# An attention product and a LoRA product on one core: the opening, the x loads' queue and the place of a few steps

## The chip, the cores and the metric

The kernel runs on one core of a Trainium2 chip. Engines of a core run side by side and meet in semaphores: TensorE (PE, with its weight loads as PEld), VectorE (DVE), ScalarE (ACT), GpSimd (POOL), and SyncE (SP), which only issues transfers. Loads and stores run on the core's 16 DMA engines; those that SP issues are on queue q1, those that POOL issues on q0. The metric is the time of one execution in microseconds.

## What is computed

For each of two batches: x is layer-normalised, rounded to integers 0 to 255, and multiplied with a context matrix rounded the same way; the result is added to x. Then the sum is normalised again and goes through a dense layer with a bias and two low-rank (LoRA) corrections, which is added too.

```python
def fake_quant(x, scale, zp):
    q = jnp.clip(jnp.round(x / scale + zp), 0.0, 255.0)
    return (q - zp) * scale
# x (2, 1024, 2048), ctx (2, 2048, 2048), kernel (2048, 2048), 4 of 8 gate rows for each batch
x = x + fake_quant(layernorm(x)) @ fake_quant(ctx)
y = layernorm(x)
x = x + y @ kernel + bias + B_eff @ (A_eff @ y) + lora_B_shared @ (lora_A_shared @ y)
```

## The kernel before

Each batch has 1024 rows, in 8 tiles (t) of 128; the 2048 output columns are 4 blocks (j) of 512; the 2048 deep inner dimension is 4 groups (g) of four 128 x 128 steps. Tile t has PSUM bank t. The first product takes bf16 integers (16 matmuls of 512 columns a tile and block); the second splits both sides into a high and a low fp16 half and takes three matmuls a step (48 a tile and block).

All orders are written out by hand, one program for each engine, and every hand-over is a semaphore. What matters here:

- **The opening** (batch 0, block 0). POOL issues x tiles 0 to 3, then makes the identity and some patterns, then takes roots of variances (`root_one`, `root_pair`). VectorE takes statistics of a tile (`stats1`), its variance (`variance`), scale and shift (`scale_rows`, six small dependent steps for one tile, or for two tiles side by side). ScalarE applies them (`relu_rows`), VectorE rounds (`round1`). Tiles 0 to 3 are turned by TensorE through PSUM (`turn`, copied out by `turn_out`), tiles 4 to 7 by a DMA that SP issues (`turn_q`). Ctx groups 0 and 1 come over SP into the two halves of `stage`, groups 2 and 3 over POOL (`load_head`); ScalarE converts them (`conv_ctx`, `conv_head`) and VectorE rounds them. `first_block` is TensorE's order. A column term (`column_term`, one matmul a tile) closes each tile of batch 0; it needs a row made from the sum over the ctx block (`column_sum`, ScalarE, then VectorE's `column_low`). The products with lora_A and lora_B follow.
- **The last block of the first product** (`first_by_tile`). Its last two tiles (`tail`) run group by group, so that ring slots of the early groups come free sooner. Meanwhile VectorE evicts tiles (`evict1`), normalises and splits the first rows (`norm2`, `low2`), and makes the low halves of the first weight block (`w_group`) after ScalarE's high halves (`conv_w`); SP turns the rows (`turn_high`, `turn_low`) and loads weight groups into `stage`.
- **The second product** starts with `base0_pair` (tiles 0 and 1, group by group) and then one tile after another; the four products with the A matrix of a gate (`lora_in`, 32 matmuls of 256 columns) stand between tiles, the first after the pair.
- **The next batch's x.** While weight blocks 2 and 3 of batch 0 run, batch 1's tiles pass through the one buffer `xn`: load, statistics and normalising (`norm_next`, VectorE), quantising (`quantise_next`, ScalarE), a store to a scratch tensor. Three tiles belong to a block. `load_next_x` issues the load on POOL, between POOL's bias additions (`add_bias`, eight a block) and stores. ScalarE converts the next weight block only after the three tiles.

## Time and profile before

| | us |
|---|---|
| three timed runs | 1040.86, 1041.74, 1045.02 (median 1041.74) |
| the profiled execution | 1042.47 |
| its span, first to last instruction | 1040.9 |
| TensorE busy | 992.6 (95%) |
| VectorE busy | 539.1 (52%) |
| ScalarE busy | 296.1 (28%) |
| GpSimd busy | 216.1 (21%) |
| mean granted TensorE clock | 0.994 of full speed |

Busy shares are means over stages that differ; where TensorE is busy nearly always, a change is worth what it takes out of TensorE's waits. A wait is read from the list of waits (who waited for whom, in total), placed with the timeline, and followed back: what did the instruction that ended it wait for? The granted clock is read by windows; 1.00 is 2.4 GHz, 0.50 is 1.2 GHz.

### The profile page before, as it was taken

The page shows a single profiled execution, that of the slowest core. Times are in us where ns is not written, and L with a number is a line of the kernel's source. Part 1 is how long each engine was busy: PE and PEld are TensorE (multiplying, and loading weights), DVE is VectorE, ACT ScalarE, POOL GpSimd, SP SyncE. Part 2 cuts the span into 40 slices and gives each one's busy share as a digit, 9 for nine tenths or more (in the row PEclk, how much of TensorE's full clock was granted, in tenths as well). Part 3 has the DMA queues.
Part 4 walks back from the last instruction along what each step waited for, and adds up shares of the span by engine and source line. Part 5 has one row for each costly group of instructions (what it writes and reads, how often), then busy time and mean ns, then how long its engine had stood idle before and what let it go on. Part 6 is the DMA issues. An engine that isn't in the chain of part 4 may idle for free.

```text
span 1040.9 us, 11977 instructions
## 1 busy us (share of the span) xinstructions
PE 992.6 (95%) x4640; PEld 460.9 (44%) x4663; DVE 539.1 (52%) x757; ACT 296.1 (28%) x213; POOL 216.1 (21%) x231
## 2 busy tenths in 40 slices
PE   2899999899999989999999999989999999999997
...
GB/s 364 295 247 366 392 295 29 171 163 194 192 223 162 111 167 177 173 146 207 252 261 284 322 198 84 108 145 165 224 118 162 31 101 161 20 33 149 11 31 40
DMA packets 140138, 181.48 MB, mean 174 GB/s; under 512 B 112704, under 2 KB 112960, under 8 KB 127552
## 3 DMA queue, kind: packets, MB, share of 16 engines
...
q0 software_dynamic: 13472, 58.20, 15.7%
...
## 4 chain that ended last, share of the span: by engine, by line
PE 62%; DVE 13%; DMA 8%; ACT 6%; issue 6%; POOL 3%; SPq 0%; DVEq 0%; POOLq 0%; ACTq 0%
PE psum L1029 17%; PE psum L1224 13%; PE psum L1226 13%; PE psum L1225 13%; DMA xn<-in_x 3%; DMA stage<-in_w 3%; POOL x L655 2%; DVE ring L1495 2%; PE psum L1247 2%; DVE hl L1541 2%; ACT ring L807 1%; DMA lhs<-in_lora_b 1%; PE psum L1091 1%; DVE stats L1521 1%; DVE stats L1406 1%
## 5 line engine op out<-in xcount | busy, mean ns | idle before, releaser
L1224 PE MATMUL psum<-ring,lhs 128*128 128x512 f16 x1000 | 379.6, 380 | 8.4 <-DVE ring L1495 7.3
L1226 PE MATMUL psum<-ring,lhs 128*128 128x512 f16 x1000 | 379.8, 380 | 0.0
L1225 PE MATMUL psum<-ring,lhs 128*128 128x512 f16 x1000 | 379.7, 380 | 0.0
L1029 PE MATMUL psum<-ring,lhs 128*128 128x512 bf16 x1002 | 226.8, 382 | 4.5 <-DVE ring L1461 2.0
L1029 PEld LDWEIGHTS psum<-ring,lhs 128*128 128x128 bf16 x1024 | 100.4, 98 | 126.5 <-issue 5.1
L1224 PEld LDWEIGHTS psum<-ring,lhs 128*128 128x128 f16 x1000 | 98.0, 98 | 129.1 <-DVE ring L1495 10.4
L1226 PEld LDWEIGHTS psum<-ring,lhs 128*128 128x128 f16 x1000 | 98.0, 98 | 118.4 <-issue 0.6
L1225 PEld LDWEIGHTS psum<-ring,lhs 128*128 128x128 f16 x1000 | 98.0, 98 | 116.7 <-issue 0.8
L1548 DVE SCALAR_TENSOR_TENSOR x<-psum,sc,x 128x512 f32 (+1 forms) x63 | 44.6, 746 | 194.0 <-PE psum L1236 193.2
L655 POOL TENSOR_TENSOR x<-x,bias_sb 128x512 f32<-128x512 f32 (+1 forms) x64 | 94.0, 1492 | 153.0 <-ACT x L938 123.9
L807 ACT ACTIVATE ring<-stage,sc 128x2048 f16<-128x2048 f32 x32 | 63.6, 1999 | 198.0 <-PE psum L1226 137.5
L1495 DVE SCALAR_TENSOR_TENSOR ring<-stage,sc,ring 128x2048 f16<-128x2048 f32 x32 | 75.0, 2349 | 64.2 <-ACT ring L807 60.8
L795 ACT ACTIVATE ring<-stage,pats_sb,sc 128x2048 int16<-128x2048 f32 x30 | 62.5, 2091 | 88.8 <-DMA stage<-in_ctx_in 47.3
L674 POOL DMA_DIRECT2D out<-x x48 | 26.4, 551 | 236.8 <-DVE x L1548 221.8
L1509 DVE SCALAR_TENSOR_TENSOR x<-psum,sc,x 128x512 f32<-128x512 f32 x64 | 45.3, 743 | 28.4 <-PE psum L1029 12.8
L629 POOL TENSOR_TENSOR x<-x,bias_sb 128x512 f32<-128x512 f32 x32 | 47.3, 1512 | 41.4 <-ACT bias_sb L934 41.4
L1461 DVE TENSOR_SCALAR ring<-ring 128x2048 bf16<-128x2048 int16 x30 | 23.6, 787 | 41.7 <-ACT ring L795 41.5
L1379 DVE BATCH_NORM_STATS2 stats<-xn 128x6 f32<-128x512 f32 x32 | 19.8, 680 | 48.7 <-DMA xn<-in_x 48.6
L783 ACT ACTIVATE hl<-xn 128x2048 f16<-128x2048 f32 x16 | 30.5, 1909 | 44.5 <-DVE xn L1531 42.1
L1541 DVE TENSOR_TENSOR hl<-xn,hl 128x2048 f16<-128x2048 f32 x16 | 36.9, 2304 | 9.1 <-ACT hl L783 8.6
L1501 DVE SCALAR_TENSOR_TENSOR b_st<-stage,sc,b_st 64x1024 f16<-64x1024 f32 x16 | 23.6, 1484 | 33.8 <-ACT b_st L814 33.7
L732 POOL DMA_DIRECT2D out<-x x14 | 7.7, 547 | 121.5 <-DVE x L1548 121.1
...
## 6 DMA issues: line engine op xcount, KB each, us to landing
stage<-in_w SPq DMA_DIRECT2D x38, 1024.0 KB, 7.1
stage<-in_ctx_in SPq DMA_DIRECT2D x30, 1024.0 KB, 7.5
...
x<-in_x POOLq DMA_DIRECT2D x8, 1024.0 KB, 11.8
xn<-in_x POOLq DMA_DIRECT2D x8, 1024.0 KB, 8.0
...
lhs<-in_lora_a POOLq DMA_DIRECT2D x4, 1024.0 KB, 10.0
lhs<-in_lora_b SPq DMA_DIRECT2D x4, 1024.0 KB, 10.2
```

The source lines that it names most:

```text
L629: pool.tensor_tensor(v, v, bias_sb[:, :], ALU.add).then_inc(with_col, 1)
L655: pool.tensor_tensor(v, v, bias_sb[:, :], ALU.add).then_inc(biased, 1)
L795: act.activation(ring_i[:, g, j % 2, :, :], stage[:, i % 2, :, :], ACT.Relu, bias=Z2, scale=IS2).then_inc(act_conv, 1)
L807: act.activation(ring[:, g, 0, :, :], stage[:, i % 2, :, :], ACT.Copy, scale=of_block(CW0, j)).then_inc(act_conv, 1)
L1029: last = pe.matmul(psum[:, t, :], lhs_q[:, k, t * P:(t + 1) * P], ring_q[:, g, j % 2, u, :], start=(k == 0), stop=(k == KT - 1 and not by_pe))
L1224: pe.matmul(psum[:, t, :], hi, ring[:, g, 0, u, :], start=(kk == 0), stop=False)
L1225: pe.matmul(psum[:, t, :], hi, ring[:, g, 1, u, :], start=False, stop=False)
L1226: last = pe.matmul(psum[:, t, :], lo, ring[:, g, 0, u, :], start=False, stop=False)
L1495: dve.scalar_tensor_tensor(out=ring[:, g, 1, :, :], in0=stage[:, half_w(b, g), :, :], scalar=of_block(CW0, j), in1=ring[:, g, 0, :, :], op ...
L1509: dve.scalar_tensor_tensor(out=v, in0=psum[:, t, :], scalar=S12, in1=v, op0=ALU.mult, op1=ALU.add).then_inc(evicted, 1)
L1541: dve.tensor_tensor(hl[:, 1, :], xn[:, :], hl[:, 0, :], ALU.subtract).then_inc(y_lo, 1)
L1548: dve.scalar_tensor_tensor(out=v, in0=psum[:, t, :], scalar=of_block(INVS0, j), in1=v, op0=ALU.mult, op1=ALU.add).then_inc(evicted, 1)
```

## The change

In the opening, x tile 0 is loaded in two halves with a semaphore each; its statistics, ReLU, rounding and turning go by halves. Ctx group 0 moves from SP's queue to POOL's, between x tiles 1 and 2, with a semaphore of its own (`first_in`; `landed` corrects the counts of the other). Each tile gets its own root and its own scale step, with one dependent step fewer (`scale_row`), and the orders of VectorE, ScalarE and TensorE are written anew around that. The column terms of the first block begin after tile 5 instead of tile 4. In the last block of the first product `tail` is 4 instead of 2, for both batches; VectorE's evictions of tiles 2 and 3 stand behind the weight groups; the first `lora_in` stands inside the pair, ahead of group 3. The loads of the next batch's x move from POOL to SP.

```diff
...
             sp.wait_ge(x_in[1], 16)
-            load_ctx(0, 0, [0, 1])
+            load_ctx(0, 0, [1])
...
+            def load_next_x(b, t):
+
+                sp.wait_ge(q_rows, t + SUMS * b)
+                if not isinstance(t, int):
+                    sp.sem_inc(go_sp, 1)
+                sp.dma_start(xn[:, :], x_tile[b][bass.ds(t, 1), :, :].rearrange("a p d -> p (a d)")).then_inc(x_next, 16)
...
+                    for t in range(LNL + 1, TILES):
+                        load_next_x(b, t)
...
+                if b + 1 < NBATCH:
+                    sp.wait_ge(y_lo, TILES * (b + 1))
                 with sp.Fori(2, NBLK) as j:
                     if b == 0:
+                        load_next_x(b + 1, LNB * (j - 2))
                         w_peaks_block(j)
-                    w_block(b, j)
+                        w_block(b, j, [0, 1])
+                        for i in range(1, LNB):
+                            load_next_x(b + 1, LNB * (j - 2) + i)
+                        w_block(b, j, [2, 3])
+                    else:
+                        w_block(b, j)
                     load_b(b, j, 0)
                     load_b(b, j, 1)
+                if b + 1 < NBATCH:
+                    load_next_x(b + 1, LNL)
...
-            def root_pair(p):
-                pool.wait_ge(pair_var, p + 2)
-                pool.tensor_tensor(ROOT2, VEPS2, NEG_HALF, ALU.pow).then_inc(pair_root, 1)
-
-            load_x(range(4))
+                c = i % 2
+                pool.tensor_tensor(ROOT2[:, c:c + 1], VEPS2[:, c:c + 1], NEG_HALF[:, c:c + 1], ALU.pow).then_inc(pair_root, 1)
+
+            pool.dma_start(x2[:, 0, 0:D // 2], x_tile[0, 0, :, 0:D // 2]).then_inc(x_half, 16)
+            pool.dma_start(x2[:, 0, D // 2:D], x_tile[0, 0, :, D // 2:D]).then_inc(x_in[0], 16)
+            load_x([1])
+            pool.dma_start(stage[:, 0, :, :], ctx_v[0, 0, 0]).then_inc(first_in, 16)
+            load_x([2, 3])
...
+            root_one(2)
+            root_one(3)
...
-                if b + 1 < NBATCH:
-
-                    pool.wait_ge(y_lo, TILES * (b + 1))
                 with pool.Fori(1, NBLK - 1) as j:
-                    if b + 1 < NBATCH:
-                        load_next_x(b + 1, LNB * (j - 1))
                     add_bias(b, j, j + blk2(b, 0), True)
                     next_bias(j, j + blk2(b, 0))
-                    if b + 1 < NBATCH:
-                        for i in range(1, LNB):
-                            load_next_x(b + 1, LNB * (j - 1) + i)
                     if b == 0:
                         pool.wait_ge(red_in, j + 4)
                         pool.sem_inc(go, 1)
                         pool.partition_all_reduce(PW_W, MX_W, P, RED.max).then_inc(red_out, 1)
                     store(b, j, j + blk(b, 1, 0))
-                if b + 1 < NBATCH:
-                    load_next_x(b + 1, LNL)
                 add_bias(b, NBLK - 1, blk2(b, NBLK - 1), True)
-                if b + 1 < NBATCH:
-                    for t in range(LNL + 1, TILES):
-                        load_next_x(b + 1, t)
...
+            def relu_half(h):
+                act.wait_ge(normed, 1)
+                cols = slice(h * D // 2, (h + 1) * D // 2)
+                act.activation(q_ints[0][:, cols], x2[:, 0, cols], ACT.Relu, bias=tile_col(SHIFT1, 0),
+                               scale=tile_col(SCALE1, 0)).then_inc(relued if h else half_relued, 1)
...
-            relu_rows(0)
-            relu_rows(1)
+            relu_half(0)
+            relu_half(1)
             turn_out(0, range(2))
             ctx_block(0, 0, [0])
+            relu_rows(1)
+            ctx_block(0, 0, [1])
             turn_out(1, range(2))
-            ctx_block(0, 0, [1])
             relu_rows(2)
+            conv_head(2)
             relu_rows(3)
             turn_out(2, [0])
-            conv_head(2)
+            conv_head(3)
             turn_out(3, [0])
...
                     pe.wait_ge(ident_ready, 1)
-                pe.wait_ge(rounded, t + 1)
                 for h in range(2):
+                    if t == 0 and h == 0:
+                        pe.wait_ge(half_rounded, 1)
+                    else:
+                        pe.wait_ge(rounded, t + 1)
...
+                ring_ready(0, 0, 0)
+                tile_start(0, 0, 0)
+                group1(0, 0, 0, True)
                 turn(1)
+                ring_ready(0, 0, 1)
+                group1(0, 0, 1, True)
+                tile_start(0, 0, 1)
                 for g in range(2):
-                    ring_ready(0, 0, g)
-                    for t in range(2):
-                        if g == 0:
-                            tile_start(0, 0, t)
-                        group1(0, t, g, True)
+                    group1(0, 1, g, True)
                 turn(2)
+                ring_ready(0, 0, 2)
+                for t in range(2):
+                    group1(0, t, 2, True)
                 turn(3)
-                for t in range(2, PT):
-                    tile_start(0, 0, t)
-                    for g in range(2):
-                        group1(0, t, g, True)
-                for g in range(2, NG):
-                    ring_ready(0, 0, g)
-                    for t in range(PT):
-                        group1(0, t, g, True)
+                tile_start(0, 0, 2)
+                for g in range(3):
+                    group1(0, 2, g, True)
+                tile_start(0, 0, 3)
+                for g in range(3):
+                    group1(0, 3, g, True)
+                ring_ready(0, 0, 3)
+                for t in range(PT):
+                    group1(0, t, 3, True)
                 column_sum(0, 0)
...
-                    column_term(0, range(t + 1) if t == PT else [t])
+                    if t > PT:
+                        column_term(0, range(t + 1) if t == PT + 1 else [t])
...
-                tail = 2 if j == NBLK - 1 else 0
+                tail = 4 if j == NBLK - 1 else 0
...
+                    lora_in(b, 0)
                     pe.wait_ge(converted, grp_w(b, 0, 3) + 1)
...
-                lora_in(b, 0)
...
+            def scale_row(t):
+
+                i = t % 2
+                root, veps, t2, scale, shift = [v[:, i:i + 1] for v in (
+                    ROOT2, VEPS2, T2, pair_cols(SCALE1, t // 2), pair_cols(SHIFT1, t // 2))]
+                dve.wait_ge(pair_var, t + 1)
+                dve.wait_ge(pair_root, t + 1)
+                then(dve.scalar_tensor_tensor(out=t2, in0=root, scalar=root, in1=veps, op0=ALU.mult, op1=ALU.mult))
+                then(dve.tensor_scalar(t2, t2, 0.5, -1.5, ALU.mult, ALU.add))
+                then(dve.scalar_tensor_tensor(out=t2, in0=root, scalar=IS1, in1=t2, op0=ALU.mult, op1=ALU.mult))
+                dve.tensor_scalar(scale, t2, -1.0, None, ALU.mult)
+                dve.tensor_scalar(shift, MV2[:, i:i + 1, 0], t2, Z1, ALU.mult, ALU.add).then_inc(normed, 1)
+                dve.wait_ge(normed, t + 1)
+
+            def round_half(h):
+                cols = slice(h * D // 2, (h + 1) * D // 2)
+                dve.wait_ge(relued if h else half_relued, 1)
+                dve.tensor_scalar(q_slots[0][:, cols], q_ints[0][:, cols], 255.0, -CENTRE,
+                                  ALU.min, ALU.add).then_inc(rounded if h else half_rounded, 1)
...
-            stats1(0)
+            stats1(0, range(2))
+            stats1(0, range(2, NBLK))
             variance([0])
+            scale_row(0)
             stats1(1, range(2))
-            scale_rows([0], 0)
-            stats1(1, range(2, NBLK))
+            round_half(0)
+            stats1(1, [2])
+            round_half(1)
+            stats1(1, [3])
             variance([1])
-            round1(0)
             stats1(2, range(2))
-            scale_rows([1], 1)
+            scale_row(1)
+            ctx_group(0, 0, 0)
             stats1(2, range(2, NBLK))
+            variance([2])
             round1(1)
...
+            round1(4)
             stats1(6, range(2))
-            round1(4)
+            scale_row(5)
             stats1(6, range(2, NBLK))
+            variance([6])
             round1(5)
-            stats1(7)
-            variance([6, 7])
-            scale_rows([6, 7], 4)
+            stats1(7, range(2))
+            scale_row(6)
+            stats1(7, range(2, NBLK))
+            variance([7])
             round1(6)
+            scale_row(7)
             round1(7)
...
-                evict1(b, j, 2)
                 norm2(b, 1)
-                evict1(b, j, 3)
                 w_group(b, 0, 0)
                 low2(b, 1)
                 w_group(b, 0, 1)
-                evict1(b, j, 4)
-                evict1(b, j, 5)
-                evict1(b, j, 6)
-                evict1(b, j, 7)
+                for t in range(2, TILES):
+                    evict1(b, j, t)
...
```

VectorE in the opening, tiles 6 and 7 (before; `stats` and `sc` are small tables, `ring` here holds the tile's integers):

```order
L1406 BN_STATS stats<-x 128x6 x4
L1414 BN_AGGR sc<-stats 128x2 x2
L1415 TENSOR_SCALAR sc<-sc 128x2
L1424 TENSOR_TENSOR sc<-sc 128x2
L1425 TENSOR_TENSOR sc<-sc 128x2
L1426 TENSOR_SCALAR sc<-sc 128x2
L1428 SCALAR_TENSOR_TENSOR sc<-sc 128x2
L1429 TENSOR_TENSOR sc<-sc 128x2
L1430 TENSOR_SCALAR sc<-sc,pats_sb 128x2
L1435 TENSOR_SCALAR ring<-ring 128x2048 x2
```

and VectorE at tiles 6 and 7 now:

```order
L1440 BN_STATS stats<-x 128x6 x2
L1458 SCALAR_TENSOR_TENSOR sc<-sc 128x1
L1459 TENSOR_SCALAR sc<-sc 128x1
L1460 SCALAR_TENSOR_TENSOR sc<-sc 128x1
L1461 TENSOR_SCALAR sc<-sc 128x1
L1462 TENSOR_SCALAR sc<-sc,pats_sb 128x1
L1440 BN_STATS stats<-x 128x6 x2
L1448 BN_AGGR sc<-stats 128x2
L1449 TENSOR_SCALAR sc<-sc 128x1
L1473 TENSOR_SCALAR ring<-ring 128x2048
L1458 SCALAR_TENSOR_TENSOR sc<-sc 128x1
```

Two tiles' statistics, one scale step for both and two roundings have become half a tile's statistics, a scale step, the other half, the variance and a rounding, over and over.

TensorE in the pair that opens the second product, after weight group 1 (before, then now; `ap_st` is the A matrix, L1204 and L1235 are weight group 2's high half, L1210 and L1241 its low half, L1224 and L1255 group 3):

```order
L1204 MATMUL psum<-ring,lhs 128x512 x16
L1210 MATMUL psum<-ring,lhs 128x512 x8
L1224 MATMUL psum<-ring,lhs 128x512
L1225 MATMUL psum<-ring,lhs 128x512
L1226 MATMUL psum<-ring,lhs 128x512
L1224 MATMUL psum<-ring,lhs 128x512
```

```order
L1235 MATMUL psum<-ring,lhs 128x512 x16
L1241 MATMUL psum<-ring,lhs 128x512 x8
L1278 MATMUL psum<-lhs,ap_st 128x256 x32
L1255 MATMUL psum<-ring,lhs 128x512
L1256 MATMUL psum<-ring,lhs 128x512
L1257 MATMUL psum<-ring,lhs 128x512
```

The 32 matmuls on the A matrix now stand ahead of group 3.

SP inside the loop over weight blocks 2 and 3, at the loads of weight groups 0 to 3 (before, then now; `REGISTER_ALU` and `ISA` rows are address and semaphore work of the sequencer):

```order
L465 DMA stage<-in_w 128x2048
L461 REGISTER_ALU
L465 ISA
L465 DMA stage<-in_w 128x2048
L461 REGISTER_ALU
L465 DMA stage<-in_w 128x2048
```

```order
L474 DMA stage<-in_w 128x2048
L470 REGISTER_ALU
L474 ISA
L474 DMA stage<-in_w 128x2048
L490 REGISTER_ALU
L493 ISA
L493 DMA xn<-in_x 128x2048
L490 REGISTER_ALU
L493 ISA
L493 DMA xn<-in_x 128x2048
L470 REGISTER_ALU
L474 DMA stage<-in_w 128x2048
```

Two x loads, each with its wait for a quantised tile, stand between weight group 1 and weight group 2; a third stands at the loop's head.

## Rows read from the trace of the kernel before

**Rows 1.** TensorE's waits: line waited for, us in total, times, longest.
```profile
PE psum L1116 <- DVE hl L1435: 15.0, 1, 15.0
PE psum L1224 <- DVE ring L1495: 7.3, 5, 2.6
```

**Rows 2.** Timeline of the opening: start us, us, engine, line, operation, [idle before].
```profile
1.52 2.27 POOL L560 DMA_DIRECT2D x<-in_x  x4 [0.83 <-POOLq L1915]
4.90 0.50 DVE L1738 CAST bias_sb<-bias_sb 128x128 bf16<-128x128 f32 x1 [0.19 <-POOL bias_sb L576]
6.75 2.47 DVE L1406 BATCH_NORM_STATS2 stats<-x 128x6 f32<-128x512 f32 x4 [1.06 <-DMA x<-in_x]
12.07 2.09 ACT L743 ACTIVATE hl<-x,sc 128x2048 int16<-128x2048 f32 x1 [7.12 <-DVE sc L1430]
...
23.98 3.60 PE L1029 MATMUL psum<-ring,lhs 128*128 128x512 bf16 x8 [1.71 <-DVE ring L1461]
47.83 0.16 DVE L1424 TENSOR_TENSOR sc<-sc 128x2 f32<-128x2 f32 x1 [0.87 <-POOL sc L571]
49.14 4.08 ACT L743 ACTIVATE ring<-x,sc 128x2048 int16<-128x2048 f32 x2 [6.16 <-DVE sc L1430]
53.25 0.69 DVE L1435 TENSOR_SCALAR ring<-ring 128x2048 bf16<-128x2048 int16 x1 [1.22 <-ACT ring L743]
54.79 1.25 PE L1064 MATMUL psum<-bias_sb,ones 128*128 128x512 f16 x5 [1.25 <-DVE bias_sb L1456]
66.88 13.90 PE L1091 MATMUL psum<-lhs,pats_sb 128*128 128x512 f32 x32
```

**Rows 3.** DMA issues of 3.3 to 4 us and 52 to 54: KB, us to landing.
```profile
x<-in_x POOLq DMA_DIRECT2D x1, 1024.0 KB, 12.1
...
lhs<-ring SPq DMA_TRANSPOSE x1, 4.6
```

**Rows 4.** Timeline, batch 0, start of the second product, ScalarE and TensorE.
```profile
197.51 2.00 ACT L807 ACTIVATE ring<-stage,sc 128x2048 f16<-128x2048 f32 x1 [12.98 <-DMA stage<-in_w]
...
206.42 0.39 PE L1224 MATMUL psum<-ring,lhs 128*128 128x512 f16 x1 [1.50 <-DVE ring L1495]
211.61 3.66 PE L1247 MATMUL psum<-lhs,ap_st 128*128 128x256 f16 x32
226.14 0.38 PE L1224 MATMUL psum<-ring,lhs 128*128 128x512 f16 x1 [0.52 <-issue]
```

**Rows 5.** Timeline, batch 1, the same place, VectorE and SP.
```profile
664.66 2.35 DVE L1495 SCALAR_TENSOR_TENSOR ring<-stage,sc,ring 128x2048 f16<-128x2048 f32 x1 [2.97 <-PE psum L1029]
...
670.99 1.71 SPq L465 DMA_DIRECT2D stage<-in_w  x2
```

**Rows 6.** DMA issues of 672 to 674 us, the A matrix.
```profile
ap_st<-a_scratch SPq DMA_TRANSPOSE x1, 11.3
```

**Rows 7.** Timeline, boundaries of weight blocks 2 and 3, batch 0.
```profile
316.01 11.82 POOL L655 TENSOR_TENSOR x<-x,bias_sb 128x512 f32 x8 [10.53 <-issue]
...
329.76 0.54 POOL L611 DMA_DIRECT2D xn<-in_x  x1 [0.43 <-issue]
...
341.76 2.47 DVE L1379 BATCH_NORM_STATS2 stats<-xn 128x6 f32<-128x512 f32 x4 [10.68 <-DMA xn<-in_x]
...
372.62 3.90 ACT L807 ACTIVATE ring<-stage,sc 128x2048 f16<-128x2048 f32 x2 [1.32 <-issue]
...
387.35 0.39 PE L1224 MATMUL psum<-ring,lhs 128*128 128x512 f16 x1 [2.61 <-DVE ring L1495]
...
479.63 0.39 PE L1224 MATMUL psum<-ring,lhs 128*128 128x512 f16 x1 [1.48 <-DVE ring L1495]
```

**Rows 8.** Windows: us, TensorE busy, granted clock, DMA share, GB/s.
```profile
68.00:72.00 4.00, 4.00 (x10) 1.00 0.10 12
...
92.00:94.00 2.00, 2.00 (x4) 0.50 0.85 352
...
388.00:390.00 2.00, 2.00 (x6) 0.50 0.56 157
```

79 lines of the change are left out of this document (37 added, 42 removed).

## The prediction

> **What bounds the kernel now.** I read the granted clock first, then TensorE's own waits, then the places where they fall. TensorE is busy 992.6 of the 1040.9 us span, so the kernel is a stream of matmuls with holes, and the change can only act on the holes. The list of TensorE's waits shows the two largest: 15.0 us before its first instruction, and 7.3 us in five waits for VectorE's half of a weight group [rows 1]. Placed in time, these are four stretches. The opening, 0 to 66.9 us, ends where the lora_A products start [rows 2]. At the start of the second product of either batch, weight groups 2 and 3 come late [rows 4] (batch 1 repeats the pattern at 679.8 and 688.7). At the boundary of weight blocks 2 and 3 of batch 0 TensorE waits 2.61 us and 1.48 us [rows 7]. The fourth, the 1.99 us wait in the lora_B products, the change does not address. The granted clock was 0.50 (the lower level, 1.2 GHz) in 388 to 390 us, just after the 2.61 us wait, and there 2 us of stream held 6 matmuls [rows 8]; at the upper level they start 0.216 us apart. That wait thus costs more than itself: ten matmuls from 387.6 to 391.2 us at 0.43 instead of 0.22 us, 2.0 us.
>
> **Part 1, the opening.** I replayed the five engines' orders by hand with the durations of the rows, first for the kernel before (the replay puts the lora_A products at 67.6 us, the trace at 66.9, so it is some 0.7 us late), then for the changed order.
> Tile 0 in halves: four loads took POOL 2.27 us, 0.57 each [rows 2]. There are now six in front of the identity, so VectorE's cast of the identity moves from 4.90 to about 6.0 and its statistics from 6.75 to about 7.0. The first half landing early is therefore worth nothing; VectorE is not there to read it. The scale chain then waits for POOL's root alone and has five steps instead of six (six took 49.14 - 47.83 = 1.31 us [rows 2], so 1.1): ReLU of tile 0 can start at 11.7 instead of 12.07. ReLU in two halves of 1.05 us (half of 2.09) with the roundings between them lets TensorE begin at 13.4 instead of 15.04.
> First ctx group on the x queue: it is fourth there, ahead of x tiles 2 and 3. The fourth transfer of that queue was issued at 3.25 and landed 12.1 us later [rows 3]; x tile 2 now has that place, and its issue is later too, so it lands near 15.7. VectorE wants it at 15.4. ctx group 0 is there before ScalarE is free (16.4), so the first products run near 19.5 instead of 23.98.
> The ring rule of the Trainium skill's page "DMA: Bandwidth & Descriptors" (section "Queues, rings and completion order") speaks against this: one queue's ring starts its descriptors in order, while different queues share the engines in turn, so tile 2 pays for a whole ctx group. No row of before separates order from sharing. By sharing alone tile 2 would land near 11.6 and the opening would be some 0.3 us better.
> A scale per tile: for tiles 4 to 7 each tile now goes through half its successor's statistics (1.3), the scale (1.1), ReLU (2.09) and rounding (0.69) in a ring, 5.0 us a tile with handoffs. Roundings end at 41.0, 46.0, 51.0 and 54.8 us. Before, with pairs, the last ends at 53.25 + 0.69 = 53.9 [rows 2]. The turning DMA lands 4.6 us after its issue [rows 3], so tiles are ready at 45.7, 50.7, 55.7 and 59.5. TensorE, whose column sum now ends near 45.6 instead of 49.9, waits 1.5 us for tile 5. The column term that cost the 1.25 us wait at 54.79 [rows 2] is put off by a tile, but TensorE reaches it at 54.2 and its low row is ready at 55.5: the wait is not gone, it is the same 1.3 us. From there six terms (1.3), tile 6, tile 7 and their terms (7.3) give 64.1 against 67.6 in the replay: 3.5 us. I take **3.0**, because the ring of four tiles has more handoffs than the replay prices. Its bounds are 0.5 above nothing and 4: one more microsecond for tile 2 and half a microsecond per tile on the DMA turns leave 0.5.
> Is it kept to 187 us? The lora_B loads wait for TensorE's own products, and the DMA engines were busy only 0.10 of 68 to 72 us [rows 8], so that train of transfers starts when TensorE says so and moves with it. I keep all 3.0.
>
> **Part 2, the start of the second product.** The tail of the last attention block now runs four tiles group by group instead of two. Group 0 of the ring is released 24 matmuls earlier (5.2 us), group 1 16 matmuls (3.5 us); the block's end does not move. In batch 1 VectorE waited 2.97 us for exactly this release, up to 664.66 [rows 5]; with two evictions also put behind it, the low half of weight group 1 and the issue of weight loads 2 and 3 at 670.99 come 2.2 us earlier (what is then last is the second tile's low half behind its turn). In batch 0 there was no such wait; only the two evictions at 0.67 us each go, so 1.2 us. ScalarE started group 2 at 197.51, released by a load [rows 4], and at 679.8 in batch 1 likewise; both move with it. The 1.13 us wait in batch 0 shrinks to about 0.5, the 1.29 us in batch 1 goes.
> The lora product moved ahead of group 3 (32 matmuls, 3.66 us) is pulled into the 1.50 us wait at 206.42 [rows 4] and its like in batch 1 at 688.7; group 3 is then ready before TensorE asks. The product needs its A matrix: issued at 672.8, landed 11.3 us later at 684.1 [rows 6], now about 681.9, and TensorE arrives at 687.2 - 0.3 - 1.3 = 685.6. Cover 3.7 us; in batch 0 it is 3.3.
> What is late next is tile 3: TensorE waited 0.52 us for its turned halves at 226.14 already [rows 4], and they hang on VectorE's chain, which moves only by 1.2 and 2.2 us. Anything above that which TensorE gains it gives back there. So **1.2** in batch 0 and **2.0** in batch 1. Bounds: 0 (the chain does not move) and 3.3 and 3.1 (all waits of the stretch).
>
> **Part 3, the x loads of the next batch on SP's queue.** On POOL they stood behind work: POOL's eight bias adds ran 316.01 to 327.8, the load was issued at 329.76, and VectorE's statistics waited 10.68 us for it, to 341.76 [rows 7]. Through two such tiles ScalarE is done quantising only at 371.3 and starts weight group 0 at 372.62, and group 2 reaches TensorE at 387.3, 2.61 us late [rows 7]. On SP the first load goes out at 302.9 instead of 304.95 with nothing ahead of it and lands near 309.5 instead of 316.5. The second waits for the quantised tile (322) and for VectorE's maxima (324.1), is issued at 324.6 behind two weight loads and lands by 333, 8.8 us early. The third then lands near 350.6, and quantising ends near 362. Group 0's ring slot is only released 15.5 us before the block's end at 379.6, at 364.1, so ScalarE is no longer what is late. Group 2: load issued 368.5, landed 374.3, both halves done by 379, wanted at 384.8. Group 3: 384 against 387.4. Both waits should close: 2.6 + 2.0 (clock) + 1.5 = **6.1**. What is queued behind the new waits on SP are weight loads 2 and 3, which need group 0 converted anyway, and that is later than the quantising. Lower bound 0, if the x load behind the weight loads is as slow as the 12.0 us it took before. POOL loses the loads; its bias adds start sooner, and nobody waits for them.
> Nothing else has a price: the semaphores' new counts and the wait for y_lo on SP pass when reached.
>
> **Sum.** 3.0 + 1.2 + 6.1 + 2.0 = 12.3 us. The profiled execution took 1042.47 us (1.57 outside its span), 0.7 above the median of the three timed runs, inside their 1040.86 to 1045.02. 1042.5 - 12.3 = **1030.2 us**.
>
> **Rivals.**
> A, the forecast, 1030.2 (1027 to 1033): 45%.
> B, the opening gives nothing: x tile 2 late, the one-tile ring as slow as the pairs, new short holes of TensorE at the lower clock. For it: tile 5's rounding is later than now (46.0 against 43.8). 1030.2 + 3 to 5, 1034: 20%.
> C, everything closes: 3.5 + 3.3 + 6.1 + 3.1, and the lora_B stall no longer drops the clock (in 92 to 94 us it stood at 0.50 [rows 8]; four matmuls at 0.88 for 0.43, 1.8 us): 17.8 off, 1024.7: 12%. Against it: VectorE's chain at tile 3.
> D, the boundary waits stay, since three x loads share SP's ring with six weight loads and the one at 329.76 took 12.0 us beside weight loads already. 1030.2 + 6.1 = 1036.3: 13%. By the ring rule of the same page of the Trainium skill this is the likelier way for the second tile to be late, since it must start after both weight loads.
> E, the other side: the A matrix is turned by a DMA behind two weight loads and TensorE now stands at its product with group 3's matmuls queued behind. It decides once the landing is more than 3.3 us later than I have it; at twice 11.3 us the stall is 7.6 us and 2 us of clock in each batch: 1030.2 + 19 = 1049: 4%.
> F, the change doesn't do what it says, the order moves but the same waits end last: 1041: 6%.
>
> **How the numbers follow.** A measurement here can tell about 0.5% from no change, 5.2 us, so faster means below 1036.5. A, B and C lie there with 77%, and D half: 84% faster. F, the other half of D: 12% the same. E: 4%. The range takes in A to D: 1024.5 to 1037.
>
> **What would show it.** Opening: lora_A products start near 63.9; TensorE's first instruction near 13.4; if the first is above 66, B. Second product: no VectorE wait for the ring before group 0 in batch 1, the A product between groups 2 and 3 without a wait; a wait of 1 to 2 us at tile 3. Boundaries: no wait near 376 and 463, the granted clock 1.00 there, x loads landing in 6 to 9 us. A wait of several us before the lora product would be E. The forecast is wrong above all if the x loads on SP's queue take 12 us.

## The result, and the profile after

The changed kernel took 1031.22 us (median of four runs, 1030.22 to 1032.51) against 1042.53 for the kernel before on the same chip: a ratio of 0.9891 with a 95% interval of 0.9874 to 0.9907. The forecast was 1030.2. Measured again later (experiment 11) it took 1034.53, ratio 0.9929 (0.9908 to 0.9950); why it varies so is part of what follows. The profiled execution took 1032.13 us, its span is 1030.6; TensorE is busy 990.9 of it.

TensorE's largest waits (as [rows 1]):

```profile
PE psum L1140 <- DVE hl L1468: 13.4, 1, 13.4
PE psum L1050 <- DVE ring L1499: 4.0, 1, 4.0
PE psum L1255 <- issue: 2.1, 1, 2.1
PE psum L1085 <- DVE bias_sb L1494: 2.0, 1, 2.0
PE psum L1235 <- ACT ring L827: 1.4, 1, 1.4
```

The first wait shrank from 15.0 to 13.4 us, and the 7.3 us for weight groups are gone. All holes of TensorE over 0.1 us add up to 39.5 us before and 31.0 after.

Where it went is best seen by cutting the span at three rows that both kernels have: the first matmul of the second product of batch 0, the matmul near 301 us that waits for a weight group of block 1, and the first matmul of the second product of batch 1. The four stretches and what the forecast gave each:

| stretch | before | after | gained | forecast |
|---|---|---|---|---|
| 1: start to second product, batch 0 | 187.05 | 186.94 | 0.1 | 3.0 |
| 2: to the mark near 301 | 113.78 | 114.08 | -0.3 | 1.2 |
| 3: to second product, batch 1 | 368.74 | 362.61 | 6.1 | 6.1 |
| 4: to the end | 371.33 | 366.97 | 4.4 | 2.0 |
| span | 1040.9 | 1030.6 | 10.3 | 12.3 |

So the time was nearly right and its parts were not: one of four is right, one came out at twice its forecast, and two brought nothing.

**Stretch 1.** TensorE's timeline (start us, us, engine, line, operation, [idle before]), then SP's (answers [rows 2]):

```profile
13.35 2.08 PE L1140 MATMUL psum<-bias_sb,hl 128*128 128x128 bf16 x16 [13.35 <-DVE hl L1468]
19.46 1.89 PE L1050 MATMUL psum<-ring,lhs 128*128 128x512 bf16 x4 [4.03 <-DVE ring L1499]
...
50.26 3.63 PE L1050 MATMUL psum<-ring,lhs 128*128 128x512 bf16 x15 [1.06 <-DMA lhs<-ap_st]
55.84 1.88 PE L1085 MATMUL psum<-bias_sb,ones 128*128 128x512 f16 x6 [1.95 <-DVE bias_sb L1494]
58.74 6.00 PE L1050 MATMUL psum<-ring,lhs 128*128 128x512 bf16 x16 [1.02 <-DMA lhs<-ring]
...
68.47 10.03 PE L1112 MATMUL psum<-lhs,pats_sb 128*128 128x512 f32 x23
```

```profile
47.89 1.49 SPq L395 DMA_DIRECT2D stage<-in_ctx_in  x2
50.92 7.95 SPq L367 DMA_TRANSPOSE lhs<-ring  x2
```

The start is as forecast: first matmul 13.35 (13.4), first products 19.46 (19.5), VectorE's wait for x tile 2 0.94 us. So are the roundings: tile 6's ended at 50.89 and tile 7's at 54.99 (51.0 and 54.8). Then tile 6 is turned at 58.7 instead of 55.7. From the DMA issues of 47 to 51.5 us (KB, us to landing):

```profile
stage<-in_ctx_in SPq DMA_DIRECT2D x2, 1024.0 KB, 6.9
lhs<-ring SPq DMA_TRANSPOSE x1, 7.8
```

Tile 6's turn took 7.8 us, not the 4.6 of [rows 3]: it was issued at 50.92 behind two ctx loads on the same queue, which took 6.1 and 7.7 us and landed at 54.0 and 56.7; the turn landed 2.0 us behind the second. Before, the ctx loads went out 1.5 us earlier (46.39) and landed at 52.0 and 54.8, and the turn 1.1 us later (52.06): it too landed 1.9 us behind the second load, at 56.7, and so the 4.6 us. Three waits (1.06, 1.95, 1.02 us) within 10 us were then followed by the lower clock; windows of 56 to 62 us (engine busy times, granted clock, DMA share, GB/s):

```profile
56.00:58.00 2.00, 1.72 (x6) 0.39 (x4) 2.00 (x1) 1.91 (x3) 0.00 (x0) 0.69 1.23 259
58.00:60.00 2.00, 1.26 (x4) 0.43 (x5) 2.00 (x2) 1.91 (x3) 0.57 (x1) 0.50 1.14 222
60.00:62.00 2.00, 2.00 (x6) 0.73 (x5) 2.00 (x2) 1.91 (x3) 0.53 (x1) 0.50 0.82 157
```

Granted 0.50 is 1.2 GHz: 6 matmuls in 2 us instead of 11 (60 to 62 us). The lora_A products start at 68.47, 1.6 us later than before, where I had 63.9. And yet the second product starts at the same time, since the lora_B products before waited 1.99 us and then ran partly at the lower clock (0.50 in 92 to 94 us [rows 8]), and here waited less and kept the clock. Before, and after:

```profile
89.64 8.83 PE L1102 MATMUL psum<-lhs,pats_sb 128*128 128x512 f32 x16 [1.99 <-DMA lhs<-in_lora_b]
```

```profile
89.73 7.19 PE L1123 MATMUL psum<-lhs,pats_sb 128*128 128x512 f32 x16 [0.50 <-DMA lhs<-in_lora_b]
```

**Stretch 2.** SP, ScalarE and TensorE at the start of the second product of batch 0 (answers [rows 4]), and the DMA issues of 188 to 191 us:

```profile
188.47 1.55 SPq L474 DMA_DIRECT2D stage<-in_w  x2
...
197.37 2.00 ACT L827 ACTIVATE ring<-stage,sc 128x2048 f16<-128x2048 f32 x1 [13.59 <-DMA stage<-in_w]
...
199.42 3.63 PE L1235 MATMUL psum<-ring,lhs 128*128 128x512 f16 x16 [1.36 <-ACT ring L827]
...
225.94 0.38 PE L1255 MATMUL psum<-ring,lhs 128*128 128x512 f16 x1 [2.13 <-issue]
```

```profile
stage<-in_w SPq DMA_DIRECT2D x2, 1024.0 KB, 9.4
bias_sb<-in_bias POOLq DMA_DIRECT2D x1, 256.0 KB, 7.6
lhs<-hl SPq DMA_TRANSPOSE x1, 7.9
```

The same place before, the issues of 187 to 188.5 us:

```profile
bias_sb<-in_bias POOLq DMA_DIRECT2D x1, 256.0 KB, 3.9
lhs<-hl SPq DMA_TRANSPOSE x1, 7.0
```

The turn of the low half went out 1.3 us earlier (186.46 against 187.73), the weight loads 2 and 3 behind it 2.8 us earlier (188.47 against 191.30). But the turn landed only 0.4 us earlier (194.4 against 194.7), and ScalarE could take the first load at the same time (197.37 against 197.51), in either kernel some 3 us behind the turn. The wait of 1.50 us at group 3 is gone, and the one at tile 3 grew from 0.52 to 2.13.

**Stretch 3.** SP, VectorE and ScalarE at the boundary of weight block 2 (answers [rows 7]), and a window (answers [rows 8]):

```profile
303.21 0.37 SPq L493 DMA_DIRECT2D xn<-in_x  x1
...
312.38 2.47 DVE L1410 BATCH_NORM_STATS2 stats<-xn 128x6 f32<-128x512 f32 x4 [4.22 <-DMA xn<-in_x]
...
336.39 2.47 DVE L1410 BATCH_NORM_STATS2 stats<-xn 128x6 f32<-128x512 f32 x4 [10.36 <-DMA xn<-in_x]
...
367.09 3.90 ACT L827 ACTIVATE ring<-stage,sc 128x2048 f16<-128x2048 f32 x2 [1.32 <-issue]
378.36 2.00 ACT L827 ACTIVATE ring<-stage,sc 128x2048 f16<-128x2048 f32 x1 [7.37 <-DMA stage<-in_w]
```

```profile
388.00:390.00 2.00, 2.00 (x11) 0.93 (x10) 0.95 (x1) 0.90 (x1) 0.00 (x0) 1.00 0.84 259
```

There is no wait of TensorE between 302 us and the end. The x loads of this block landed 9.1, 9.4 and 6.5 us after issue, only the second of them behind two weight loads; statistics of the second tile began at 336.39 instead of 341.76, and ScalarE came to weight group 0 at 367.09 instead of 372.62, in both kernels 1.3 us after it was done quantising.

**Stretch 4.** SP and ScalarE at the start of the second product of batch 1 (answers [rows 5]), and the issues of 661 to 664 us:

```profile
661.52 1.52 SPq L474 DMA_DIRECT2D stage<-in_w  x2
...
667.48 2.00 ACT L827 ACTIVATE ring<-stage,sc 128x2048 f16<-128x2048 f32 x1 [10.38 <-DMA stage<-in_w]
```

```profile
stage<-in_w SPq DMA_DIRECT2D x2, 1024.0 KB, 7.1
lhs<-hl SPq DMA_TRANSPOSE x1, 4.4
```

Against the first matmul of this product (669.57 before, 663.63 after) the loads went out 3.5 us earlier and ScalarE began group 2 6.4 us earlier. All four waits of the stretch (0.29, 1.29, 1.50, 0.50 us) are gone. They make nearly the whole 4.4 us: a wait costs 0.16 us more than its row says, since a matmul's row is 0.38 us long and in a dense stream the next one starts 0.22 us after it, so 3.6 + 4 x 0.16 = 4.2.

### The profile page after: what moved, and what is told of

The parts are those of the page before. It is cut to its first block, busy times and chain, and to the rows that moved or that the text cites. A ratio compares the mean times of both kernels' runs of the same rounds, so it can differ in the third digit from the quotient of the medians.

```text
span 1030.6 us, 12010 instructions
## 1 busy us (share of the span) xinstructions
PE 990.9 (96%) x4639; PEld 460.5 (45%) x4663; DVE 540.3 (52%) x771; ACT 297.4 (29%) x214; POOL 212.9 (21%) x228
## 3 DMA queue, kind: packets, MB, share of 16 engines
q0 software_dynamic: 12608, 50.86, 13.4%
## 4 chain that ended last, share of the span: by engine, by line
PE 80%; DVE 9%; DMA 5%; ACT 4%; issue 1%; POOL 0%; DVEq 0%; SPq 0%; ACTq 0%; POOLq 0%
PE psum L1255 19%; PE psum L1257 19%; PE psum L1256 19%; PE psum L1050 17%; PE psum L1278 2%; DMA stage<-in_w 1%; DVE ring L1533 1%; DVE hl L1579 1%; PE psum L1112 1%; DMA stage<-in_ctx_in 1%; DMA x<-in_x 1%; PE psum L1267 1%; PE psum L1266 1%; DVE stats L1559 1%; DMA lhs<-ring 1%
## 5 line engine op out<-in xcount | busy, mean ns | idle before, releaser
L1255 PE MATMUL psum<-ring,lhs 128*128 128x512 f16 x1000 | 379.0, 379 | 2.7 <-issue 2.1
L1255 PEld LDWEIGHTS psum<-ring,lhs 128*128 128x128 f16 x1000 | 97.8, 98 | 120.8 <-issue 2.6
L679 POOL TENSOR_TENSOR x<-x,bias_sb 128x512 f32<-128x512 f32 (+1 forms) x64 | 91.6, 1455 | 144.4 <-ACT x L959 117.4
```

The source lines that it names most:

```text
L679: pool.tensor_tensor(v, v, bias_sb[:, :], ALU.add).then_inc(biased, 1)
L1255: pe.matmul(psum[:, t, :], hi, ring[:, g, 0, u, :], start=(kk == 0), stop=False)
```

## Experiments

Theory: the x loads on SP's queue carry stretch 3, the tail of four tiles (with the two evictions behind the weight groups) stretch 4, and what the opening and the moved A product gain is taken back at the next place that is paced by something else. Rivals: the opening is a loss, or a gain that shows later; the A product is what closes batch 1. The four stretches of every kernel, from its one profiled execution, and the start of the lora_A products inside the first:

| kernel | lora_A | 1 | 2 | 3 | 4 |
|---|---|---|---|---|---|
| before | 66.88 | 187.05 | 113.78 | 368.74 | 371.33 |
| changed | 68.47 | 186.94 | 114.08 | 362.61 | 366.97 |
| 1 old opening | 66.95 | 186.31 | 115.29 | 363.95 | 366.95 |
| 2 x on SP only | 66.94 | 186.52 | 114.00 | 362.61 | 371.27 |
| 3 ctx behind turns | 66.14 | 185.76 | 114.17 | 362.61 | 366.96 |
| 4 and terms late | 67.92 | 188.79 | 114.12 | 362.61 | 366.98 |
| 5 second product only | 66.80 | 186.42 | 114.77 | 368.39 | 367.02 |
| 6 A product only | 66.80 | 186.67 | 114.42 | 369.69 | 372.82 |
| 7 opening only | 65.83 | 185.97 | 113.68 | 369.08 | 371.37 |
| 8 changed, tile 2 early | 66.15 | 186.07 | 112.91 | 362.61 | 367.01 |
| 9 and quiet turns | 63.76 | 186.59 | 112.23 | 362.61 | 366.97 |
| 10 as 8, old opening | 66.92 | 187.47 | 112.85 | 363.17 | 366.91 |
| 11 changed, again | 68.38 | 188.79 | 114.83 | 362.66 | 366.92 |
| 12 tail only | 66.93 | 187.11 | 114.58 | 368.91 | 367.10 |

Stretches 3 and 4 take one of two values, to a few tenths, by one part of the change each: 362.6 to 364.0 with the x loads on SP and 368.4 to 369.7 without; 367.0 with the tail of four and 371.3 to 372.8 without. Stretches 1 and 2 are less sure: the changed kernel's own two executions (changed, 11) lie 1.85 and 0.75 us apart there, 0.05 in the other two.

**1, the old opening under the rest of the change, and 2, the x loads alone.**

```diff
 # 1: changed kernel, opening (queues, halves, scale per tile, orders) as before
-            load_ctx(0, 0, [1])
+            load_ctx(0, 0, [0, 1])
 # 2: kernel before, with only
+                        load_next_x(b + 1, LNB * (j - 2))      # SP, and gone from POOL
+                        w_block(b, j, [0, 1])
+                        for i in range(1, LNB):
+                            load_next_x(b + 1, LNB * (j - 2) + i)
+                        w_block(b, j, [2, 3])
```

> The changed kernel with the opening of before: only the second product's start and the x loads on SP's queue are changed. Theory 1 (the new opening is worth nothing to the end: TensorE reaches the lora_A products 1.6 us later, 68.5 against 66.9, and gets that back in the lora_B products, where its wait shrank from 1.99 to 0.50 us and the clock stayed up): about 1031.2, within 0.7 of the changed kernel; lora_A products at 66.9, a wait near 2 us at 89.6. Rival 2 (the 1.6 us are lost to the end): 1029.6. Rival 3 (the opening did bring its 3 us somewhere behind 100 us): 1033 to 1034.

Measured 1032.54 (ratio 0.9915, 0.9899 to 0.9932). That is 1.3 us over the changed kernel's 1031.22, outside theory 1 and short of rival 3, and the intervals of the two ratios overlap: the time decides nothing. In the profiled execution a wait of 1.17 us at block 2 stayed, and a wait of 2.13 us at 195.5 us was followed by the lower clock (0.60 and 0.54 in 196 to 200 us), hence the long stretch 2; in stretch 1 the old opening is no slower.

> The kernel before with nothing but the next batch's x loads moved to SP's queue. Theory 1 (the waits at weight blocks 2 and 3 of batch 0 close and nothing else moves: 2.6 + 2.0 of clock + 1.5 = 6.1): 1042.5 - 6.1 = 1036.4, and the four waits at the start of the second product of batch 1 (0.29, 1.29, 1.49, 0.50) stay. Rival 2 (these waits of batch 1 also go, since the x loads no longer delay what stands in front of them): 1032.9. Rival 3 (they only close together with the tail of four tiles): above 1040.

Measured 1036.14 (0.9955, 0.9939 to 0.9972), 5.5 us under before: theory 1. Three of batch 1's four waits stayed (1.80, 1.50, 0.47 us):

```profile
675.46 3.63 PE L1205 MATMUL psum<-ring,lhs 128*128 128x512 f16 x16 [1.80 <-ACT ring L808]
682.30 0.39 PE L1225 MATMUL psum<-ring,lhs 128*128 128x512 f16 x1 [1.50 <-DVE ring L1496]
```

**3 and 4, the turns of tiles 6 and 7.** Edits to the changed kernel:

```diff
-            for t in range(PT, TILES - 2):
+            for t in range(PT, TILES):          # 3 and 4: all four turns, then the ctx loads
                 turn_q(t)
             load_ctx(0, 1, [0, 1])
-                    if t > PT:
+                    if t > PT + 1:              # 4 only: column terms from tile 6 on
```

> The changed kernel with ctx groups 0 and 1 of block 1 loaded behind the turning DMAs of tiles 6 and 7 instead of ahead of them. Theory 1 (tile 6's turn took 7.8 us instead of 4.6 because two ctx loads stood ahead of it; TensorE's waits of 1.55, 1.95 and 1.02 us in 10 us then dropped the clock to 0.50 from 57 to 63 us): tile 6 is ready at 55.5, no wait for it, the clock stays at 1.00, the lora_A products start at 68.5 - 1.0 - 2.7 = 64.8, and the kernel is at 1027.5 if that is kept. Rival 2 (the clock falls all the same, because of the waits for tile 5 and the column term): 67.5 and 1030.2. Rival 3 (all is given back in the lora_B wait or the next column sum, since the loads of ctx and lora_B come later): 64.8 and 1031.2.

Measured 1031.58 (0.9914, 0.9894 to 0.9933). Tile 6 was turned in 4.3 us and TensorE did not wait for it, so the two loads issued ahead of it are the cause of the 7.8 us. The clock fell all the same (0.50 in 58 to 60 us), after waits of 1.06 and 1.95 us (the 1.55 of the expectation was 1.06 in the changed kernel too). The lora_A products started 2.3 us earlier than in the changed kernel; the wait for lora_B grew from 0.50 to 1.63 us and half of the 2.3 was gone. Rival 2 as to the clock, and half of rival 3; the half that arrived, 1.2 us, is less than the changed kernel's own 1.85.

> The run before (ctx loads behind the turns) and also the column terms put off by one more tile, until after tile 6. Theory 1 (the wait of 1.95 us for the column term's row goes, as the row is ready at 55.8 and TensorE asks at 57.5 or later): lora_A products at 62.9, the kernel 1.9 us under the one before it, 1025.6 if kept. Rival 2 (TensorE then only waits for tile 6 or tile 7, ready at 55.5 and 59.5): 63.5 to 64.8, under 1 us. Rival 3 (given back behind the lora_A products): no change of the time.

Measured 1033.68 (0.9922, 0.9905 to 0.9939). The column term no longer waited, but now tile 7 did, 2.21 us up to 62.55. Its turn took 7.5 us. The issues of 52 to 56 us (two turns, of tiles 6 and 7, 4.3 and 7.5 us, median 5.9; in 3 the two took 4.3 and 7.5 us as well):

```profile
lhs<-in_lora_a POOLq DMA_DIRECT2D x1, 1024.0 KB, 8.3
lhs<-ring SPq DMA_TRANSPOSE x2, 5.9
```

Here the loads beside tile 7's turn were issued behind it (it went out at 55.0): one of lora_A on the other queue (55.45), two of ctx in its own ring (from 56.44). The wait of 2.21 us was followed by the lower clock (0.50 in 64 to 66 us), which none of the three had, the lora_B products then waited 3.02 us, and the second product started at 188.79, as late as in 11. What was forecast as a gain was none; the time, 2.1 us over 3's with overlapping intervals, doesn't show a loss either.

**5, 6 and 12, the start of the second product in parts**, each on the kernel before.

```diff
 # 5 and 12
-                tail = 2 if j == NBLK - 1 else 0
+                tail = 4 if j == NBLK - 1 else 0
-                evict1(b, j, 2)                 # and 3: behind w_group(b, 0, 1)
 # 5 and 6
+                    lora_in(b, 0)               # in the pair, ahead of group 3
```

> The kernel before with only the changes at the start of the second product (tail of four tiles, evictions behind the weight groups, the A product ahead of group 3). Theory 1 (in batch 0 the three waits of 0.7, 1.1, 1.5 us only move to tile 3; in batch 1 all four, 3.6 us, go; the boundary waits of blocks 2 and 3 stay): 1041.7 - 3.6 = 1038.1. Rival 2 (batch 0 gives its 1.2 as well): 1036.9. Rival 3 (batch 1's waits closed in the changed kernel only because the x loads had left their old place): above 1040.

Measured 1038.45 (0.9967, 0.9956 to 0.9977): theory 1. Batch 1 has no wait, batch 0 one of 2.13 us at tile 3.

> The kernel before with only the A product moved ahead of weight group 3. Theory 1 (it closes the waits of 1.50 and 1.49 us at group 3 and both come back at tile 3, where VectorE's chain has not moved): waits at tile 3 near 2.0 us in both batches, the time 1041.7 as before. Rival 2 (tile 3 had cover, the 3.0 us are kept): 1038.7. Rival 3 (the A matrix lands too late and TensorE waits at its product): 1043 or more.

Measured 1043.70 (1.0011, 0.9997 to 1.0024), no difference from before that is clear: theory 1 as to the waits. TensorE at tile 3 in batch 0, and in batch 1 at group 2 and at tile 3:

```profile
225.37 0.58 PE L1224 MATMUL psum<-ring,lhs 128*128 128x512 f16 x1 [2.18 <-issue]
...
682.93 3.63 PE L1204 MATMUL psum<-ring,lhs 128*128 128x512 f16 x16 [1.63 <-ACT ring L807]
...
709.46 0.38 PE L1224 MATMUL psum<-ring,lhs 128*128 128x512 f16 x1 [2.14 <-issue]
```

The two waits of 1.5 us at group 3 are gone and those at tile 3 are 2.18 and 2.14 instead of 0.52 and 0.50: moved, and 0.15 us more. Both were followed by the lower clock (0.50 in 226 to 228 and 710 to 712 us), so that stretch 4 is 1.5 us longer than before. The time is in rival 3's range, but not by its mechanism: the A matrix was never waited for.

> The kernel before with the tail of four tiles and the evictions behind the weight groups, and the A product left where it was. Theory 1 (in batch 1 it is the earlier release of ring group 0 that closes the waits, all of them: group 3's low half was ready 676.3 in the changed kernel, and TensorE without the A product in front asks for it at 663.6 + 16.1 = 679.7; in batch 0, where VectorE never waited for that release, nothing changes): batch 1's 3.6 us go, batch 0 keeps its waits of 1.1 and 1.5 us, the time 1041.9 - 3.6 = 1038.3, the same as with the A product moved. Rival 2 (without the A product in between the wait of 1.5 us at group 3 stays in batch 1): 1039.8. Rival 3 (the A product was what counted): 1041.9.

Measured 1038.30 (0.9961, 0.9939 to 0.9982): theory 1. Batch 1 has no wait at all without the A product's move; batch 0 kept 1.39 and 1.50:

```profile
199.43 3.63 PE L1204 MATMUL psum<-ring,lhs 128*128 128x512 f16 x16 [1.39 <-ACT ring L807]
...
206.28 0.39 PE L1224 MATMUL psum<-ring,lhs 128*128 128x512 f16 x1 [1.50 <-DVE ring L1495]
```

The tail and the two evictions were not tried apart. In batch 1 VectorE waited 2.97 us for the release [rows 5], so the evictions by themselves would have lengthened that wait; this is argued, not shown.

**7, the opening alone**, on the kernel before: all of part 1 (halves of tile 0, `first_in`, `scale_row`, the orders) and nothing else.

```diff
-            load_x(range(4))
+            pool.dma_start(x2[:, 0, 0:D // 2], x_tile[0, 0, :, 0:D // 2]).then_inc(x_half, 16)
...
+            pool.dma_start(stage[:, 0, :, :], ctx_v[0, 0, 0]).then_inc(first_in, 16)
```

> The kernel before with only the new opening. Theory 1 (the stretch of 72 to 98 us runs at the pace of its transfers, so what TensorE gains or loses ahead of it is mostly evened out): the lora_A products start near 68.5 instead of 66.9, but the second product of batch 0 starts at 187.0 within 0.7 of before, and the time is 1041.7 within 1. Rival 2 (the forecast's 3 us arrive): 1038.7. Rival 3 (the late start is kept): 1043.3.

Measured 1042.04 (0.9997, 0.9984 to 1.0010): no difference, and with 10 runs against 25 the surest word on the opening: the interval leaves it at most 1.7 us, not 3.0. The start of lora_A was not 68.5 but 65.83, which none of the three had. The same opening, nearly the same three waits (1.09, 1.93, 1.28 us), and the clock stayed up; windows, then TensorE's wait in the lora_B products:

```profile
58.00:60.00 2.00, 1.52 (x7) 0.70 (x8) 2.00 (x1) 1.91 (x3) 0.57 (x1) 1.00 1.13 214
60.00:62.00 2.00, 2.00 (x11) 0.93 (x10) 2.00 (x2) 1.91 (x3) 0.53 (x1) 1.00 0.77 210
```

```profile
87.98 7.38 PE L1122 MATMUL psum<-lhs,pats_sb 128*128 128x512 f32 x16 [1.39 <-DMA lhs<-in_lora_b]
```

It reached lora_A 1.05 us before the kernel before, and the wait for lora_B is 1.39 us: at the second product (185.97) it is 0.3 us ahead of the earliest of the old openings (186.31 to 187.47).

**8, the wait at tile 3.** VectorE stood idle for 3.89 us in front of weight group 2, with tile 2's normalising queued behind it. Edit to the changed kernel, both batches:

```diff
                 stats2(b, 2)
-                w_group(b, 0, 2)
                 norm2(b, 2)
+                w_group(b, 0, 2)
                 w_group(b, 0, 3)
 # ScalarE: root(b, 1, 2) ahead of w_groups(b, 0, [2])
```

> The changed kernel with tile 2's root and normalising ahead of weight group 2 instead of behind it, on ScalarE and VectorE, in both batches. Theory 1 (VectorE stands idle for 3.89 us up to 199.4 in batch 0, as weight group 2's load lands late; the 2.3 us of normalising fit in, its chain moves 1.9 us forward and the wait of 2.13 us at tile 3 shrinks to 0.3): 1031.2 - 1.8 = 1029.4. Rival 2 (the waits behind it, 0.66 us at 262.6 and 0.60 us at 301.0, take it back): 1031.2. Rival 3 (in batch 1, where VectorE has only 1.0 us of idle time there, the low half of group 2 comes 1.3 us later and TensorE waits for it): 1030.7 or more.

Measured 1028.91 (1028.46 to 1030.12; 0.9870, 0.9853 to 0.9886), under the changed kernel's 1031.22 and the lowest median of the study; the two intervals overlap. Theory 1. VectorE, then TensorE at tile 3:

```profile
194.93 0.16 DVE L1420 RECIPROCAL sc<-sc 128x1 f32<-128x1 f32 x1 [0.27 <-ACT sc L750]
199.62 2.35 DVE L1533 SCALAR_TENSOR_TENSOR ring<-stage,sc,ring 128x2048 f16<-128x2048 f32 x1 [2.40 <-ACT ring L827]
...
224.28 0.38 PE L1255 MATMUL psum<-ring,lhs 128*128 128x512 f16 x1 [0.25 <-issue]
```

VectorE's idle time is 2.40 instead of 3.89 us and the wait at tile 3 is 0.25 instead of 2.13. Stretch 2 is 1.2 us shorter, not 1.8: the turn of the low half took 9.2 us here and TensorE waited 1.69 us for it at 194.8 instead of 0.42. The single executions agree beyond their spread: the three kernels with this move (8, 9, 10) have 112.2 to 112.9 in stretch 2, the five that have the rest of part 2 and 3 without it (changed, 1, 3, 4, 11) 114.1 to 115.3.

**9, 10 and 11.** 9 adds to 8 an opening in which no load runs beside the turns of tiles 6 and 7; 10 is 8 with the old opening; 11 is the changed kernel unaltered, on the chip of 9 and 10.

```diff
 # 9, on top of 8 and the edits of 3 and 4
+            sp.wait_ge(q_turned[TILES - 1], 16)       # before load_ctx(0, 1, [0, 1])
+            pool.wait_ge(q_turned[TILES - 1], 16)     # before lora_A chunk 2
```

> The version with tile 2's normalising early, and an opening in which nothing shares the DMA engines with the turns of tiles 6 and 7: ctx groups 0 and 1 of block 1 and lora_A chunk 2 are issued once tile 7 is turned, and the column terms begin after tile 6. Theory 1 (the opening can be shortened, but 72 to 98 us runs at the pace of its transfers and now has 3 MB more to move after 59 us): lora_A products at 64.0 instead of 66.1, a wait for lora_B of 3 to 4 us instead of 1.76, the second product of batch 0 at 186.1 within 0.7, the time 1028.9 within 1. Rival 2 (the 2.1 us are kept): 1026.8. Rival 3 (the transfers pushed back cost more than they free): 1030 or more.

Measured 1030.19 (0.9893, 0.9876 to 0.9911). Both turns took 4.2 and 4.3 us, the column terms waited for nothing, and the lora_A products started at 63.76, as forecast for the whole change. Then:

```profile
89.22 8.83 PE L1123 MATMUL psum<-lhs,pats_sb 128*128 128x512 f32 x16 [3.08 <-DMA lhs<-in_lora_b]
```

3.08 us of waiting for lora_B, and 16 matmuls in 8.83 us, partly at the lower clock (0.50 in 90 to 92 us); the second product starts at 186.59. By the profile theory 1: the stretch of the lora products is paced by its transfers. The time is 0.3 us beyond its bound and in the range of rival 3, on another chip than 8.

> The version with tile 2's normalising early and the opening of before. Theory 1 (the new opening is worth under 1 us: in runs whose clock stayed up there it reached the second product of batch 0 at 185.97 and 186.07, the old one at 186.31 to 186.67 and 187.05): 1028.9 + 0.5 = 1029.4, and the wait of 1.2 us at block 2 may return, as it did with the old opening before. Rival 2 (it is worth the 3.0 us of the forecast): 1031.9. Rival 3 (nothing or less): 1028.9 or under.

Measured 1030.75 (0.9895, 0.9879 to 0.9912), against 1030.19 of 9 on the same chip: no difference that can be told. Against 8's 1028.91, on another chip, it lies midway between theory 1 and rival 2 and decides neither; in the traces 8 is 1.4 us ahead at the second product, where the clock fell in 10's lora_B products and not in 8's, and 0.6 us in stretch 3, where the wait at block 2 is back with 0.39 us. Over all profiled executions the old opening (seven) reaches the second product at 186.79 on average, the new one (changed, 7, 8, 11) at 186.94: at 185.97 and 186.07 where its clock stayed up, at 186.94 and 188.79 where it fell.

> The changed kernel itself once more. Theory 1 (the clock's fall to 0.50 from 57 to 63 us was one execution's and not the opening's: a kernel with the same opening had the same waits of 1.08, 1.93 and 1.28 us there and no fall): lora_A products at 66.0 instead of 68.5, with the same three waits; the time 1031.2 within 1. Rival 2 (the fall belongs to the changed kernel): 68.5 and the clock at 0.50 again.

Measured 1034.53 (1031.65 to 1035.55). Rival 2 as to this execution: nearly the same three waits (1.06, 1.95, 0.90) and the clock at 0.50 again, lora_A at 68.38. So the fall came in both profiled executions of the changed kernel and not in 7 and 8, which have its opening line for line. Over this kernel's eight runs the mean granted clock goes with the time: 0.995 in the runs of 1032.13, 1032.51, 1034.27, 1034.80 and 1035.55 us, 0.997 or 0.998 in those of 1030.22, 1030.31 and 1031.65. What decides it in an execution stays open. Nor is the clock the whole difference between 1031.22 and 1034.53: both profiled executions had the fall and came to lora_A within 0.1 us of each other. The first lora_B loads went out at 72.01 and 72.09 us, yet the lora_B products started at 91.39 in 11 and at 89.73 in the other; in 74 to 98 us the DMA engines moved 9.1 MB against 9.7. Why is not known.

## Where the prediction held and where it failed

**Part 3, the boundaries: right.** 6.1 us forecast, 6.1 in the stretch (experiment 2: 6.1 alone). The mechanism is the one given. The margins were thinner than worked out: first x load landed at 312.3 (forecast 309.5), second at 336.4 (by 333), ScalarE at group 0 at 367.1 (364.1), at group 2 at 378.4 (374.3). One step of it did not hold: quantising ended at 365.8, not near 362, so that ScalarE was still what group 0 waited for, and not the ring's release at 364.1. And experiments 1 and 10 have 1.17 and 0.39 us of wait left at block 2, so it closes with little to spare. Rival D is refuted: the loads took 6.5 to 9.4 us, 9.4 behind two weight loads, not 12.

**Part 2, batch 1: right in kind, mis-sized.** Forecast 2.0, measured 4.4 in the stretch, 3.6 of it in the rows of the waits. The step that failed is that VectorE's chain moves by 2.2 us only and tile 3 gives the rest back. The ring's release moved the loads 3.5 us, and the turn and the loads then met no other transfer: the turn of the low half took 4.4 us instead of 7.6 and the loads 7.1 instead of 9.4, so group 2 was 6.4 us earlier and tile 3 had cover. The credit goes to the tail with its two evictions (12); the A product's move (6) brings nothing in either batch.

**Part 2, batch 0: wrong, 1.2 forecast, nothing there.** The evictions' 1.2 us did arrive at the turn of the low half: against the first matmul of the second product it was issued 1.2 us earlier. The step that failed is that I kept them to the end and priced no change of flight. The turn took 7.9 us instead of 7.0, and the weight loads behind it in the ring, issued 2.8 us earlier, were ready when they had been before (8.9 us from issue to ScalarE instead of 6.2). In all fourteen executions of batch 0 it is the same: the four without the tail of four issue the turn later and have it in 6.9 to 7.0 us, the ten with it in 7.7 to 9.6. Where the clock didn't fall, stretch 2 has 113.7 to 114.0 us without the tail and 114.1 to 114.8 with it (experiment 8's move left aside), so the forecast gain is rather a small loss.
What shares the engines with the turn is POOL's bias load, before as after (187.51 and 187.41 us). Over both batches of the fourteen executions the turn took 6.7 to 9.6 us in the eighteen places where that load was in flight beside it, and 4.4 us in each of the ten, all in batch 1 with the tail of four, where it was issued after the turn had landed (664.51 in the changed kernel). That agrees everywhere, but the bias load was not moved by itself. The end of the term, a wait of 1 to 2 us at tile 3, came as forecast (2.13).

**Part 1, the opening: wrong, 3.0 forecast, 0.** Two steps failed.
First, "the turning DMA lands 4.6 us after its issue" was carried over from a place where the two ctx loads ahead of it had been issued 5.7 and 4.7 us before it, to one where it was 3.0 and 1.9 us. Tile 6 was ready at 58.7, not 55.7. I had weighed ring order for x tile 2 (there it held: 12.6 us from issue to landing, 12.1 forecast) and not for the turn. The Trainium skill's page "DMA: Bandwidth & Descriptors", section "Queues, rings and completion order", has both halves of what was seen: within a ring descriptors are taken in order, and between rings an engine changes over packet by packet. Experiment 3 agrees with the first (tile 6's turn: 7.8 us behind the two loads, 4.3 with none ahead). Experiment 4 agrees with the second (tile 7's turn: 7.5 us with loads of both queues in flight, 4.3 in 9 with none), but which of the two queues' loads it was isn't separated.
Second, "that train of transfers starts when TensorE says so and moves with it". It starts so: the first lora_B load is issued 3.6 us after the first lora_A product in the kernels before and after and in 9. But it lasts as long as its bytes need. From 74 to 98 us the DMA engines had hardly any idle time (share 0.97 or more in every 2 us). Two windows of the changed kernel:

```profile
80.00:90.00 10.00, 9.50 (x23) 4.07 (x22) 6.07 (x7) 3.66 (x4) 1.45 (x2) 1.00 1.01 417
90.00:98.00 8.00, 7.95 (x21) 3.29 (x22) 3.33 (x6) 2.92 (x3) 2.17 (x3) 1.00 1.01 418
```

Where lora_A started 2.3 us earlier (3) 1.2 arrived; where 2.4 (9 against 8), nothing did, though 9 had also pushed 3 MB of loads into the train. Each by itself is within the 1.85 us by which this kernel's own executions differ there; the timed runs of 7 say the same more surely. The row of 68 to 72 us that I used [rows 8] shows the train's start, and its pace stood in the rows behind.
By the sign I had set, lora_A above 66, this was rival B, and its mechanism was there in part (tile 6 late, short holes, the lower clock). Its price was not: where the lora_A products came later, the lora_B wait shrank by as much (0.50 against 1.99 us). In its repetition (11) the changed kernel did take B's time.

**Why the sum was right all the same.** By luck: errors of both signs partly cancelled. 2.9 and 1.5 us too much in stretches 1 and 2, 2.4 too little in stretch 4: 12.3 - 2.0 = 10.3 of span. In it are two falls of the clock before (1.8 and 2.0 us) and one after (68.47 against 65.83 and 66.15 in experiments 7 and 8, some 2.4 us). The forecast counted only the one at block 2. Of the rivals, E did not happen: the A matrix was never waited for.
